# Causal mask as 43 rows within the products, one head of 128 queries per maximum, one projection of q, in an adaLN attention and mixture-of-experts kernel

## The reference, cut to what matters

```python
h = layernorm(x) * (1 + ca) + sa                     # ca, sa: 128 values per batch
qkv = h @ w_attn
q = qkv[..., :128].reshape(B, T, 16, 8).transpose(0, 2, 1, 3);  k = qkv[..., 128:136];  v = qkv[..., 136:]
att = einsum('bhqd,bkd->bhqk', q, k) / sqrt(8)
att = where(tril(ones((T, T))), att, -inf)           # causal
y = einsum('bhqk,bkd->bhqd', softmax(att), v)
x = x + ga * (y @ w_proj)
h = layernorm(x) * (1 + cb) + sb                     # then 16 experts, top 4 by a sigmoid gate, and a shared one
x = x + gb * (shared + routed)
```

## Time and profile before

| | us |
|---|---|
| median of 3 runs | 452.66 (450.77 to 454.01) |
| the profiled execution | 452.19 |
| its span | 450.5 |
| TensorE (PE) busy | 394.2 |
| VectorE (DVE) busy | 271.4 |
| ScalarE (ACT) busy | 228.3 |
| GpSimd (POOL) busy | 156.0 |
| mean granted TensorE clock | 0.939 |

### The profile page before, as it was taken

The page is one execution under the profiler, slowest core; times in us unless marked ns, Lnnn a source line. Parts: engine busy times, 40 slices in busy tenths (PEclk is TensorE's granted clock), DMA queues, the critical chain, the costliest instruction groups (busy, mean ns, idle before and its releaser), DMA issues.

```text
span 450.5 us, 6135 instructions
## 1 busy us (share of the span) xinstructions
PE 394.2 (88%) x2097; PEld 182.3 (40%) x2097; DVE 271.4 (60%) x637; ACT 228.3 (51%) x421; POOL 156.0 (35%) x283
## 2 busy tenths in 40 slices
PE   7797949988799995988989998995999998866996
PEld 7464413433345442334354443332634333215542
DVE  5556945588788587777446854885268835113343
ACT  2323327656567863446367544674585546843400
POOL 4923478645621267361224130043028020202000
PEclk9958779999999997999999999999799999995999
DMA  5002700030000340030900000000170000000000
GB/s 141 1 1 62 169 0 1 2 73 1 3 0 1 98 96 0 0 71 5 187 0 25 1 1 0 24 1 1 39 152 3 1 1 23 3 0 1 0 0 25
DMA packets 15935, 13.69 MB, mean 30 GB/s; under 512 B 5728, under 2 KB 11504, under 8 KB 15904
## 3 DMA queue, kind: packets, MB, share of 16 engines
q1 hardware_dynamic: 15488, 12.90, 12.9%
q10 hardware_dynamic: 416, 0.39, 0.3%
HBM read 9.65 MB, written 1.15 MB: 24 GB/s over the span
## 4 chain that ended last, share of the span: by engine, by line
PE 65%; POOL 11%; DVE 11%; ACT 5%; issue 5%; DMA 1%; POOLq 0%; ACTq 0%; DVEq 0%
PE bank L881 61%; DVE mn L799 5%; POOL pr L581 3%; POOL xn L483 3%; ACT pr L645 2%; POOL rstd L474 1%; PE bank L1054 1%; PE bank L914 1%; POOL placer L510 1%; DMA xs<-in_L_attn_x 1%; ACT L645 1%; DVE sl L871 1%; DVE q_left L756 1%; ACT fT L681 1%; DVE stat L700 1%
## 5 line engine op out<-in xcount | busy, mean ns | idle before, releaser
L799 DVE TENSOR_REDUCE mn<-bank 128x1 f32<-128x512 f32 (+6 forms) x304 | 178.2, 627 | 78.7 <-PE bank L881 78.4
L645 ACT ACTIVATE pr<-bank 128x512 f32<-128x512 f32 x288 | 160.2, 598 | 107.8 <-PE bank L881 106.3
L881 PE MATMUL bank<-ka,qa 96*128 96x512 bf16 (+7 forms) x384 | 109.4, 335 | 8.0 <-DVE mn L799 5.6
L881 PE MATMUL bank<-qa,ka 100*128 100x512 bf16 x288 | 109.1, 389 | 2.1 <-ACT pr L645 2.0
L581 POOL TENSOR_SCALAR_AFFINE_SELECT pr<-pr 128x256 f32<-128x256 f32 x128 | 49.0, 424 | 168.2 <-ACT pr L645 168.2
L881 PE MATMUL bank<-pr,va 128*32 128x512 f32 x576 | 79.0, 622 | 9.0 <-POOL pr L581 8.2
L881 PE MATMUL bank<-hT_parts,up_parts 128*128 128x512 f32 x216 | 66.3, 439 | 5.4 <-DVE mn L799 5.0
L881 PEld LDWEIGHTS bank<-qa,ka 100*128 100x128 bf16 x288 | 27.9, 100 | 88.5 <-ACT pr L645 44.2
L881 PEld LDWEIGHTS bank<-ka,qa 96*128 96x128 bf16 x384 | 36.2, 102 | 43.3 <-DVE mn L799 19.2
L881 PEld LDWEIGHTS bank<-hT_parts,up_parts 128*128 128x128 f32 x216 | 41.3, 201 | 22.5 <-issue 7.3
L871 DVE TENSOR_TENSOR sl<-sl,bank 128x512 f32<-128x512 f32 x36 | 24.7, 687 | 25.4 <-PE bank L881 22.4
(11 more groups left out here) (139 smaller groups left out, 315.8 us busy)
## 6 DMA issues: line engine op xcount, KB each, us to landing
comb_wide<-comb_rows SPq DMA_DIRECT2D x6, 1024.0 KB, 9.9
qa<-qp SPq DMA_DIRECT2D x18, 128.0 KB, 3.8
xs<-in_L_attn_x SPq DMA_DIRECT2D x4, 256.0 KB, 5.6
out_x<-xs SPq DMA_DIRECT2D x4, 256.0 KB, 2.3
qa<-shiftT SPq DMA_DIRECT2D x32, 4.0 KB
sl<-in_L_ffn_e_win SPq DMA_DIRECT2D x1, 512.0 KB, 4.1
sl<-in_L_ffn_e_vin SPq DMA_DIRECT2D x1, 512.0 KB, 5.6
w_out<-in_L_ffn_e_wout SPq DMA_DIRECT2D x1, 512.0 KB, 5.5
```

Of the source, the lines that this page charges most:

```text
L645: act.activation(pr[:, n % NPB, g, :], s_bank[in_s[x] % NS][:, :], ACT.Exp, scale=SCALE).then_inc(s_read, 1)
L799: v.tensor_reduce(mn[:, place[u] % 2, part, hf, a, r:r + n], m_bank[k % NM][:, 0:n * w].rearrange("p (n w) -> p n w", w=w), AX.X, ALU.max, ...
L881: return pe.matmul(out, lhsT, rhs, start=start, stop=stop, skip_group_check=True)
```

## The change

**Rows.** A head has its own columns: `qa` becomes [128, 2 batches, 16 heads, 1024], with 48 rows of q (six products of 8), 43 rows of the mask (48 to 90) and two rows of the shift (91, 92). Mask row r holds at query 3r + i the value Q_MASK[i], and in `ka[:, 1]` at key j of the tile one of K_MASK by how far j lies beyond 3r, so that the product is 0 on and below the diagonal and a huge negative number above it. `ka[:, 0]` has zeros there, for tiles off the diagonal. GpSimd builds one tile of each (`q_mark`, `k_mark`) before its plan, and SyncE spreads them: one DMA per chunk of 43 rows x 16 heads x 1 KB (704 KB) for q, and one per batch for k.

**Maxima.** A job covers 128 queries of one head. `tri`, `onehot` and `in_group` go. Where a job reaches the diagonal, each head's product is in two matmuls, the plain columns and the 128 masked ones. There are 304 jobs again.

**q.** One product of 128 columns per chunk; `placer` and the "place" work go; the first chunk's q is put in place by DMAs like the others', of 8 partitions x 16 heads x 1 KB instead of 16 x 4 x 2 KB. The second chunk's hT and q now come ahead of the first maxima.

**Scores.** No affine_selects. pv waits for the exponentials alone.

**Memory.** `pr` has 2 buffers instead of 3; `combT` 1 instead of 2; `k_rest` shares its tensor with `q_left`, so `q_rest` and `k_rest` wait for each other's readers; `picker` lies in `comb_wide` and is built after the last unit's pv.

```diff
-    NS, NM, NPB = 3, 3, 3
+    NS, NM, NPB = 3, 3, 2
+    QROWS = len(PRODUCTS) * HD
+    MG = 3
+    MROWS = QROWS + (P + MG - 1) // MG
+    SROWS = MROWS + 2
+    Q_MASK = (2.0 ** 51, 1.0, 2.0 ** -51)
+    K_MASK = (0.0, -2.0 ** -27, -2.0 ** 24, -2.0 ** 75)
...
+        k0 = CH if t * P >= CH else 0
+        if k0:
+            jobs += [(u, 1, h, 1, 0, CH, False) for h in range(H)]
+        w = (t + 1) * P - k0
+        n = CH // w
+        jobs += [(u, 0, h, n, k0, w, True) for h in range(0, H, n)]
...
-    plan += [("k", c0), ("k_rest", c0), ("k_mid", c0), ("v", c0), ("k_set", c0), ("warm", 8)]
-    plan += [("place", j) for j in range(2 * NPAIR)]
+    plan += [("k", c0), ("k_rest", c0), ("k_mid", c0), ("v", c0), ("k_set", c0)]
+    side += [..., (1.0, ("marks",)), (2.0, ("fetch",)), ...]
...
+    plan += [("hT", c1), ("q", c1), ("q_rest", c1)]
     max_of(order[0])
-    plan += [("hT", c1)]
+    plan += [("k", c1), ("k_rest", c1)]
     max_of(order[1])
     through_shift(order[0])
-    plan += [("q0", c1), ("q_rest", c1, 0), ("q1", c1), ("q_rest", c1, 1), ("k", c1), ("k_rest", c1)]
+    plan += [("k_mid", c1), ("v", c1)]
     for j in range(4):
         one_max()
-    plan += [("k_mid", c1), ("v", c1)]
...
+        def mark(sp, c):
+            sp.dma_start(qa[QROWS:MROWS, b, :, t0:t0 + CH],
+                         q_marks[QROWS:MROWS, :, :]....broadcast_to([MROWS - QROWS, H, CH])).then_inc(q_marks_in[c], 16)
...
# SyncE, ahead of its plan
+            sp.wait_ge(q_marked, 1)
+            mark(sp, c0)
+            sp.wait_ge(k_marked, 1)
+            for b in range(B):
+                sp.dma_start(ka[QROWS:SROWS, 1, b, :]..., k_marks[QROWS:SROWS, :]...).then_inc(k_marks_in, 16)
...
# SyncE, in its plan
+                elif kind == "marks":
+                    for c in CHUNKS[1:]:
+                        mark(sp, c)
...
# GpSimd, ahead of its plan
+            own(gp.memset(q_mark[:, :], 0.0))
+            for i in range(MG):
+                own(gp.affine_select(out=q_mark[:, :], ..., fill=Q_MASK[i], base=MG * QROWS - i, pattern=[[1, P]], channel_multiplier=-MG))
+            gp.tensor_copy(q_marks[:, :, :], q_mark[:, :].unsqueeze(1).broadcast_to([P, 4, P])).then_inc(q_marked, 1)
+            own(gp.memset(k_mark[:, :], K_MASK[MG]))
+            # four more affine_selects and a copy, then k_marked
...
# TensorE, max
                     for i in range(n):
-                        ins = mm(to[:, i, :], qa[0:MROWS, b, r + i, 2 * q0:2 * q0 + 2 * Q],
-                                 ka[0:MROWS, hf, b, k0:k0 + w], stop=not m)
-                    if m:
-                        ins = mm(to[:, :, w - Q:w], onehot..., tri[:, :].unsqueeze(1).broadcast_to([P, n, Q]), start=False)
+                        q = qa[0:MROWS, b, h + i, t * P:(t + 1) * P]
+                        if plain:
+                            ins = mm(to[:, i, 0:plain], q, ka[0:MROWS, 0, b, k0:k0 + plain])
+                        if m:
+                            ins = mm(to[:, i, plain:w], q, ka[0:MROWS, 1, b, t * P:(t + 1) * P])
...
# TensorE, scores and pv
                     mm(s_bank[k % NS][:, :].rearrange("p (h q) -> p h q", h=HG),
+                       ka[0:SROWS, int(kt == t), b, kt * P:(kt + 1) * P],
+                       qa[0:SROWS, b, HG * g:HG * (g + 1), t * P:(t + 1) * P]).then_inc(s_ready, 1)
...
+                    pe.wait_ge(s_read, in_s["scores", n, G - 1] + 1)
                     if first:
-                        pe.wait_ge(masked, G * (place[u] + 1))
...
# VectorE
+                    v.tensor_copy(ka[0:SROWS, 0, b, t0:t0 + CH], k_all[0:SROWS, :])
+                    v.tensor_copy(ka[0:QROWS, 1, b, t0:t0 + CH], k_all[0:QROWS, :]).then_inc(k_done, 1)
```

More of the change, by code:

```diff
@@ L106, in then @@
         elif kind == "hT":
[L107 to L110, removed]
+            smalls.append((now + 1.6, ("q", a)))
+        elif kind == "q":
+            side.append((now + 1.6, ("q_rest", a)))
+            smalls.append((now + 2.6, ("k", a)))
         elif kind == "k":
@@ L130, in adaln_attention_moe_kernel @@
     first_step = [G * first_block[u] for u in order]
-    cost = [0.07 + 0.565 * j[5] * j[7] / CH for j in jobs]
+    cost = [0.07 + 0.565 * j[3] * j[5] / CH for j in jobs]
     due = []
@@ L226, in adaln_attention_moe_kernel @@
             st["up"] += 1
-        for i, g in enumerate(GORDER):
+        for i, g in enumerate(range(G)):
             if n and i == G - 1:
@@ L264, in adaln_attention_moe_kernel @@
             uses[at[x]] += 1
-    in_s = {x: n for n, x in enumerate(x for x in plan if x[0] in ("scores", "hin") or x[0] == "place" and x[1] % 2 == 0)}
-    in_m = {x: n for n, x in enumerate(x for x in plan if x[0] in ("max", "vin", "comb") or x[0] == "place" and x[1] % 2)}
+    in_s = {x: n for n, x in enumerate(x for x in plan if x[0] in ("scores", "hin"))}
+    in_m = {x: n for n, x in enumerate(x for x in plan if x[0] in ("max", "vin", "comb"))}
     gate_no = {x: n for n, x in enumerate(x for x in plan if x[0] == "gate")}
@@ L316, in adaln_attention_moe_kernel @@
         rstd = sb("rstd", [P, NU], f32)
-        qp = [sb(f"qp{i}", [Q, 2, CH, 2], bf16) for i in range(3)]
-        placer = sb("placer", [Q, 3, NPAIR, MROWS], bf16)
-        q_left = sb("q_left", [Q, CH, 2], f32)
-        qa = sb("qa", [P, B, NPAIR, 2 * T], bf16)
+        qp = [sb(f"qp{i}", [P, 2, CH], bf16) for i in range(3)]
+        q_left = sb("q_left", [P, CH], f32)
+        k_rest = q_left
+        qa = sb("qa", [P, B, H, T], bf16)
         k_all = sb("k_all", [P, CH], bf16)
         ka = sb("ka", [P, 2, B, T], bf16)
-        in_group = sb("in_group", [P, 9], f32)
+        q_marks, k_marks = sb("q_marks", [P, 4, P], bf16), sb("k_marks", [P, P], bf16)
+        q_mark, k_mark = sl[:, 4, 2 * P:3 * P], sl[:, 4, 3 * P:4 * P]
         va = sb("va", [P, NU, 32], f32)
-        mn = sb("mn", [P, 2, 2, 2, 2, NPAIR], f32)
-        shift = sb("shift", [P, 2, 2, 2, 2, NPAIR], bf16)
+        mn = sb("mn", [P, 2, 2, H], f32)
+        shift = sb("shift", [P, 2, 2, H], bf16)
         shiftT = sb("shiftT", [32, 2, P], bf16)
@@ L641, in _ @@
                     n, g = x[1:]
-                    if g == GORDER[0] and n >= NPB:
+                    if g == 0 and n >= NPB:
                         act.wait_ge(pv_done, n - NPB + 1)
```

281 lines of the change are left out of this document (95 added, 186 removed).

## The result

The changed kernel takes 541.92 us (median of four runs, 540.85 to 543.85) where the kernel before takes 451.72 beside it: a ratio of 1.199, 95% interval 1.193 to 1.206. The forecast was 431.5 us with a range up to 443. The kernel is slower by 90 us, and the error is 110 us.

A forecast was written before the change was run, and what follows sets the result against it. The prediction took TensorE's queue to bound the body, while no engine is full at the start. From 452.2 us profiled it took 14.8 up to unit 2 and 6.1 in the body: 431.3, so 431.5 us; range 423 to 443.

The forecast's parts named there:

- the part from the first score to unit 2: First score at 33 to unit 2 at 53: selects' 4.58 us wait goes, marks and weights delay the shift; 14.8 us gained so far.
- rival C: At unit 2, slow marks hold up SyncE's queue and the shift: slower than before, 455 us at 60 GB/s; chance 0.04.
- Rival A: At the start, q DMAs into 8 partitions run at 54 GB/s, first maximum at 28, total 441 us; chance 0.15.
- The wait of 2 us: At unit 2's first score, TensorE waits for the shift behind marks and weights: 2 us, range none to 13.
- The body: From unit 2 on: selects 3.3, columns 2.6, q products 1.8, less 1.6 for VectorE's reductions, a gain of 6.1 us.
- columns and q's products: In the body, less TensorE work: 8,192 fewer matmul columns save 2.6 us, one q product instead of two saves 1.8 us.
- Rival D: Selects were not what held pv; exponentials or evac as late, 435 us if half the 7.9 us stays; chance 0.05.
- the two later waits: In the body, TensorE's waits for GpSimd's selects of 0.55 us at 74.24 and 2.75 us at 121.15 go: 3.3 us.
- Rival B: VectorE becomes the body's bound: columns and q products gain nothing, 5.1 us are added, 439 us; chance 0.08.
- Rival E: Short 128-column matmuls cost more than their columns, loads not hidden: bound 15 us, half gives 439 us; chance 0.05.
- the 0.047 of the bound: In the body, the most extra us one 128-column matmul can cost beyond its columns: 15 us for 320; forecast took nothing.
- the prediction's 9 us: In the body, extra for 128-column matmuls by the Trainium skill's 81 ns each against 53 for columns; not counted in forecast.

The follow-up runs named there:

- 48 rows: The changed kernel with 48 mask rows per marks DMA instead of 43, five more of zeros: 442.47 us, ratio 0.981 to the kernel before.
- the late mark: The changed kernel with 48 mask rows, first chunk's marks DMA issued only once the wmod weights have landed: 439.93 us, ratio 0.973 to the kernel before.
- the spread q: Against the kernel with 48 mask rows and late first mark: product rows reordered so each q copy writes partitions six apart; 433.41 us, ratio 0.956.

## Why the prediction was wrong

**The step that failed** is in the part from the first score to unit 2: "marks start near 35, take 10 us at 203 GB/s". They moved 24 to 25 GB/s and took 86 us, on one engine of 16. The rival C had the mechanism (the marks stand ahead of the shift of unit 2, on one queue, and TensorE waits in order) and its formula: the marks start at 35 and take their bytes over their rate, and the weights and the landing take 8 us more. Three marks at 24.5 GB/s take 86 us. With the late start that the first mark caused, 66.5 in place of 35, the formula puts the shift at 161, and unit 2's first score came at 163.35. C was given 0.04, since I took the 203 GB/s of 16-row DMAs for a rate that any DMA reaches, three times the 65 GB/s at which C loses its 24 us. None of the rows that I read showed a DMA whose number of rows has no large divisor, and that should have widened the bound instead of closing it.

**The mark at the start** was costed at nothing. It blocked SyncE's next issue for 27 us and so q's copies, and the first maximum came 24 us later than before. The forecast counted the DMAs that the start waits for, and not the one queued ahead of them.

**q's copies** were a mis-sized term: 100 GB/s forecast (203 halved), 60 measured. Rival A had said 54 and a first maximum at 28; with 48 rows and the late mark it is 28.67, and the total 439.93 for A's 441. So once the marks are mended, A is what happened, and it had 0.15. Its details fit less well: A had the first score near 44 (41.30) and no wait at unit 2 (1.33 us).

The rule behind A, of the Trainium skill ("SBUF — State Buffer", Door 1, the DMA port swizzle), was set aside because of the 203 GB/s. By their averages the runs bear it out within about a fifth: 66 GB/s for 8 neighbouring rows where it gives 54, 128 for 16 where it gives 109, and more than twice the rate of 8 neighbouring rows once they are spread over its ports. The 203 of the earlier trace rows was the peak of a burst. In the same burst the next two microseconds show 154 and 45, and in the burst of the second chunk's copies the engines are as busy one microsecond after the peak and move half as much:

```profile
40.00:41.00 1.00, 0.00 (x0) 0.00 (x0) 0.89 (x2) 0.18 (x2) 0.91 (x2) 1.00 0.81 197
41.00:42.00 1.00, 0.69 (x4) 0.58 (x5) 1.00 (x4) 0.62 (x1) 1.00 (x1) 0.54 0.91 96
```

Over 97 to 100 the average is 134 GB/s. So the forecast halved a peak. That the peak comes from several copies to different rows being in flight together is likely, but was not tested.

**Unit 2.** The wait of 2 us that was forecast is 1.19 with 48 rows and 3.75 with the spread q, where the first score is 1 us behind the forecast. From first score to unit 2 it takes 20.0 us with 48 rows (20 forecast, 23.7 before).

**The body** was right in its sum: -6.1 us forecast from unit 2 on, -7.3 in the changed kernel (375.4 for 382.7) and -5.4 with 48 rows (377.3). These are single executions, which differ by some microseconds from run to run. The division into terms is not borne out. The forecast had 4.4 us less of TensorE's work there (columns and q's products) and 1.7 us less of waiting. Measured with 48 rows: TensorE is busy for 1.3 us less (339.7 for 341.0) and idle for 4.1 us less. By its terms:
- No wait of TensorE for GpSimd's `pr` is left. Rival D falls: without the selects alone the time falls by 7.6 us. But the 3.3 us counted for the two later waits do not show in that run, as said above; the clock behind the first wait, which the forecast left out, makes up for half of them.
- The maxima have a mean of 656 ns, as forecast. Rival B falls: with 48 rows VectorE waits 74.3 us for TensorE before the maxima, as it did before (78.7).
- Rival E falls. Four 128-column products in a row, with their loads, at a granted clock of 1.00 (TensorE's timeline of the kernel with 48 rows):

```profile
37.34 0.40 PE L850 MATMUL bank<-ka,qa 96*128 96x128 bf16 x4 [1.34 <-DVE mn L768]
37.94 0.40 PE L850 MATMUL bank<-ka,qa 96*128 96x128 bf16 x4 [0.20 <-DVE mn L768]
```

  The last three of a group start 0.055 to 0.056 us apart, and most 128-column maxima of this trace at that clock have the same distance to the next product (ahead of a pv it is 0.147). Their columns alone are 0.053. So the extra cost is about 0.003 us for most of the 320, 1 to 3 us in all (my estimate from these distances), and neither the 0.047 of the bound nor the 0.028 behind the prediction's 9 us. The 0.60 us from group to group are VectorE's pace.
- TensorE's busy time fell by 12.9 us in the changed kernel and 7.0 (394.2 to 387.2) with 48 rows, not by 17. With 48 rows the 7.0 are 5.3 up to the first maximum, 1.8 to the first score, 1.4 more than before to unit 2, and 1.3 after it. In the first three stretches the granted clock is lower than before (0.79, 0.63 and 0.62 for 0.86, 0.72 and 0.72), and the same score product takes 0.61 us at the lower level and 0.38 at the higher.

**The start to first score.** 12.6 us from the first maximum to the first score (34.05 less 21.49) where 11.5 were forecast, once the copies are fast. The chain of reasoning about the start therefore holds; the two rates in it did not. With three further edits (48 rows, the late first mark, the spread rows of q) the kernel takes 433.41 us, against a forecast of 431.5. (The sum has a slip of no weight: 431.3 plus the 0.5 us between the profiled execution and the median is 431.8.)

## What to carry to other kernels

Before a DMA is priced, look at its number of rows: 43 and 47, both primes, put all of it on one engine (24 to 25 GB/s instead of 230), and rounding up by five rows of nothing, or cutting 43 into 32 + 11, mended it. A slow transfer costs most through what is issued behind it on the same sequencer, so list that too. Where DMAs of few rows are on the path, spread the rows over the partitions, and let a rate from another shape, above all the peak of one microsecond, widen the range rather than exclude a rival. When a wait of TensorE is priced, look at the granted clock behind it too: here a wait of 4.58 us cost another 1.6 by the slower clock.

## What was not expected of the hardware

- One engine alone moves 24 to 25 GB/s, two 48. But eight engines writing eight neighbouring partitions move about 60 to 66 together, 16 writing sixteen neighbouring ones 128, and eight writing to partitions six apart 129 to 137 (averages over some microseconds).
- With a DMA on one engine ahead of it, the issue of a later one can stand: SyncE stood for 27.4 us in the issue of k's marks and for 29.0 in the fetch, though only one engine was busy. Why it stands there and not one DMA earlier, the runs do not show.
- An 8 KB transfer issued on ScalarE's queue took some 10 us behind 2.3 MB of SyncE's queue.
- 128-column products with their weight loads start 55 to 56 ns apart at a granted clock of 1.00 (the kernel with 48 rows).
